# Products that nobody reads, between the score products of the first two groups of both attention layers

## The reference

```python
x = x + _L0_attn_ref(_layernorm(x), ...)   # delta rule, 4 heads
x = x + _L0_ffn_ref(x, ...)                # holds a softmax attention of 16 heads of 8, and a mixture of 8 experts
x = x + _L1_attn_ref(_layernorm(x), ...)   # softmax attention, 32 heads of 32
x = x + _L1_ffn_ref(x, ...)                # product with a spectrum
```

```python
attn = softmax(q @ k.T * scale)            # 512 x 512 scores for each batch entry and head
o = attn @ v
```

## Time and profile before

| | us |
|---|---|
| median of 3 runs | 2050.37 |
| lowest and highest | 2046.57, 2053.72 |
| the profiled execution, its own time | 2045.67 |
| its span, first to last instruction | 2044.0 |

### The profile page before, as it was taken

The page is one execution under the profiler, slowest core; times in us unless marked ns, Lnnn a source line. Parts: engine busy times, 40 slices in busy tenths (PEclk is TensorE's granted clock), DMA queues, the critical chain, the costliest instruction groups (busy, mean ns, idle before and its releaser), DMA issues. The chain is left out here.

```text
span 2044.0 us, 49130 instructions
## 1 busy us (share of the span) xinstructions
PE 1792.3 (88%) x18950; PEld 832.5 (41%) x18950; DVE 1630.1 (80%) x3036; ACT 1285.0 (63%) x2693; POOL 1148.6 (56%) x703
## 2 busy tenths in 40 slices
PE   5537755999999955986999999999999999999997
PEld 3337733233333334663442444443443444444334
DVE  7842276999999746446878999999999999999963
ACT  5412125588888811225884777787787877777785
POOL 8722472000000037331134988989999999989995
PEclk9769958699999965998997999999999999999998
DMA  2220018111111052117994232332323223232311
GB/s 48 36 49 3 0 45 278 39 44 48 44 43 48 22 184 54 47 49 246 368 405 150 65 84 69 80 79 69 85 64 84 73 76 84 65 85 65 83 28 42
DMA packets 194495, 180.21 MB, mean 88 GB/s; under 512 B 58743, under 2 KB 155127, under 8 KB 194055
## 3 DMA queue, kind: packets, MB, share of 16 engines
q1 hardware_dynamic: 185860, 170.01, 28.6%
q0 software_dynamic: 2944, 7.10, 1.1%
q10 hardware_dynamic: 5504, 0.73, 0.2%
HBM read 101.16 MB, written 75.26 MB: 86 GB/s over the span
## 5 line engine op out<-in xcount | busy, mean ns | idle before, releaser
L972 DVE TENSOR_REDUCE maxima_l<-max_l 128x1 f32<-128x512 f32 x1024 | 651.6, 677 | 46.6 <-PE max_l L1082 40.3
L948 POOL TENSOR_TENSOR part_sums_l<-probs_l 128x1024 f32<-128x1024 f32 x256 | 615.1, 2403 | 98.3 <-ACT probs_l L1038 85.4
L1038 ACT ACTIVATE probs_l<-exp_l 128x512 f32<-128x512 f32 x1024 | 567.9, 598 | 139.6 <-PE exp_l L1093 135.5
L1082 PE MATMUL max_l<-k_stack_l,q_stack_l 96*128 96x512 f16 x1024 | 399.4, 391 | 4.1 <-DVE pv_bank_l L964 3.3
L1093 PE MATMUL exp_l<-q_stack_l,k_stack_l 100*128 100x512 f16 x1024 | 389.8, 382 | 2.5 <-ACT probs_l L1038 1.6
L1300 DVE TENSOR_REDUCE maxima_l<-max_l 128x1 f32<-128x512 f32 x512 | 316.9, 681 | 16.9 <-PE max_l L1386 16.7
L1337 ACT ACTIVATE probs_l<-exp_l 128x512 f32<-128x512 f32 x512 | 279.2, 599 | 59.6 <-PE exp_l L1399 55.9
L1127 PE MATMUL pv_bank_l<-probs_l,v_ring_l 128*32 128x512 f32 x2048 | 273.6, 606 | 0.3 <-issue 0.3
L1814 POOL IOTA rows_e<- 128x32 int32 x1 | 0.2, 183 | 386.1 <-POOLq L26 386.1
L1082 PEld LDWEIGHTS max_l<-k_stack_l,q_stack_l 96*128 96x128 f16 x1024 | 100.1, 98 | 280.1 <-DVE maxima_l L972 189.1
L979 DVE TENSOR_TENSOR part_sums_l<-part_sums_l 128x512 f32<-128x512 f32 x128 | 182.5, 1426 | 14.2 <-POOL part_sums_l L948 14.1
(11 more groups left out here) (294 smaller groups left out, 2588.6 us busy)
## 6 DMA issues: line engine op xcount, KB each, us to landing
scratch_qk_l<-parts_g SPq DMA_DIRECT2D x128, 256.0 KB, 9.3
q_stack_l<-scratch_qk_l SPq DMA_DIRECT2D x192, 128.0 KB
k_stack_l<-scratch_qk_l SPq DMA_DIRECT2D x192, 128.0 KB
scratch_v_l<-v_g SPq DMA_DIRECT2D x16, 1024.0 KB, 11.2
v_ring_l<-scratch_v_l SPq DMA_DIRECT2D x64, 256.0 KB, 3.4
scratch_stack_l<-parts_c SPq DMA_DIRECT2D x16, 384.0 KB, 3.6
q_stack_l<-scratch_stack_l SPq DMA_DIRECT2D x64, 96.0 KB, 2.2
k_stack_l<-scratch_stack_l SPq DMA_DIRECT2D x64, 96.0 KB, 2.3
```

Source lines behind the costliest of these rows:

```text
L948: pool.tensor_tensor(part_sums[:, i, h, :, :], probs[:, i, h, 0:2, :], probs[:, i, h, 2:4, :], ALU.add).then_inc(pair_sum.sem, 1)
L972: dve.reduce_max(maxima[:, s % 2, at % NT, at // NT:at // NT + 1], max_bank(n, at)[:, :], AX).then_inc(max_taken.sem, 1)
L1038: act.activation(probs[:, i, at // NT, at % NT, :], exp_ps[at % 2][:, :], ACT.Exp, scale=a.scale).then_inc(prob_tile.sem, 1)
L1082: pe.matmul(max_bank(n, at)[:, :], qs[0:SHIFT_ROW, s % RING, h, k * P:(k + 1) * P], ks[0:SHIFT_ROW, s % RING, h, :], start=True, stop=True ...
```

## The change

In steps 0 and 1, behind each score for the maxima, TensorE makes products of 384 columns from the same stacks and writes them into `exp_ps`. Nobody reads them. In L1 there are two behind each score, 64 in all. In L0 there are four behind each pair of scores, 64 in all, and all of them read the rows 0 to 47, whichever half the scores read. In L0 they count a semaphore of their own, `filled`, and TensorE waits for all 64 ahead of the first score for the exponentials. I call them fill products below.

```diff
+IDLE_FILL, IDLE_WIDTH = 2, 384
 # attention (L1), in the loop over the 16 tiles, if exists(turn, s, 0):
                         pe.matmul(max_bank(n, at)[:, :], qs[0:SHIFT_ROW, s % RING, h, k * P:(k + 1) * P],
                                   ks[0:SHIFT_ROW, s % RING, h, :], start=True, stop=True).then_inc(max_tile.sem, 1)
+                        if not exists(turn, s, EXP_LAG):
+                            for f in range(IDLE_FILL):
+                                pe.matmul(exp_ps[f % 2][:, 0:IDLE_WIDTH], qs[0:SHIFT_ROW, s % RING, h, k * P:(k + 1) * P],
+                                          ks[0:SHIFT_ROW, s % RING, h, 0:IDLE_WIDTH], start=True, stop=True)
 # attention_l0 (L0), in the loop over the 8 pairs
+        filled = sem("filled")
...
+                        if not exists(turn, s, EXP_LAG):
+                            for f in range(2 * IDLE_FILL):
+                                pe.matmul(exp_ps[f % 3][:, 0:IDLE_WIDTH], qs[0:L0_ROWS, s % RING, hh, k * P:(k + 1) * P],
+                                          ks[0:L0_ROWS, s % RING, hh, 0:IDLE_WIDTH], start=True, stop=True).then_inc(filled, 1)
                     if exists(turn, s, EXP_LAG):
                         m, slot = n - EXP_LAG, (s - EXP_LAG) % RING
                         if p == 0:
                             pe.wait_ge(shifted[slot], nth(turn, s - EXP_LAG, 16 * HALVES * NT))
+                            if not exists(turn, s, EXP_LAG + 1):
+                                pe.wait_ge(filled, 2 * IDLE_FILL * EXP_LAG * L0_PAIRS)
```

## The result

| | us | |
|---|---|---|
| before | 2049.56 | median of 11 runs (2046.57 to 2053.72) |
| after | 2058.15 | median of 11 runs (2053.71 to 2062.81) |
| ratio | 1.0042 | 95% interval 1.0031 to 1.0054: 6.4 to 11.1 us slower |
| profiled execution of after | 2059.5 | span 2057.8 (before: 2044.0) |

What follows compares the result with a forecast made beforehand. VectorE was taken to bound both layers' starts, TensorE at the low clock some later stretches. L0 (1.2 + 0.4 - 1.7 = -0.1) plus L1 (1.8 - 0.6 = +1.2) gave +1.1 us: 2051.5 from 2050.37, range 2046 to 2060.

Steps and rivals of the forecast that it cites:

- the first rival: L0: clock stays low despite the fill products, as they use 48 of 128 rows; +9.6 us, 2060.0; chance 0.13.
- The bound: Steps 0 and 1 of both layers: VectorE's reductions set the pace at 0.60 us a tile, not TensorE.
- The price of a tile or pair: TensorE with fill products at 0.50: 1.70 us an L0 pair, 1.06 an L1 tile; at 1.00, 0.55 a tile.
- how long L0's clock stays low: Start of L0: 4.2 us until the rise (ends 2.4 and 6.0), so 2.5 pairs late by 0.50, +1.2 us.
- The gain in L0: L0, start of step 3: with the clock high from step 2, VectorE's 1.93 us gap shrinks to 0.21, returning 1.7 us.
- a sign against me: Forecast wrong if the clock falls back in step 1, stays 0.50 in L0, or reductions stand over 0.60 apart at 1.00.
- the fourth rival: Larger gain: before's low clock may last longer elsewhere, about a microsecond per further L0 step 3 pair; about 2043; chance 0.04.
- the 0.6 that I took: L1, step 2: a high clock gives back the 0.6 us by which VectorE was short in 4.2.
- the bound of 1.7: L1, step 2: upper limit on the gain, TensorE's 11.3 us against 9.6 for 16 tiles.
- The shift's chain: Transposed maxima of group 0 queue behind fill products: about 0.4 us shows in L0 (0 to 0.66), nothing in L1.
- The second rival: Fill products' weight loads not overlapped: L1 tile 0.85 us at the high clock; +8.1 us in all, 2058.5; chance 0.01.
- The third: Rival: the clock rises in neither layer before step 2; 8.0 us lost in L0, 14.7 in L1, 2073; chance 0.02.

Runs made afterwards that it cites:

- l0_narrow: Kernel after without L1's fill products, L0's made 192 columns wide instead of 384, still 48 rows: 2049.8 us against 2048.64 for before, one run.
- fitted: Kernel after with one 192-column fill product per L1 tile; L0's only in step 2, one of 128 rows per pair, pairs 3 to 7: 2046.82 us against 2045.09, ratio 1.0003.
- fitted_all: As fitted, but L0's 128-row fill products stand behind all eight pairs of step 2: 2047.1 us, one run.
- l1_narrow: Kernel after without L0's fill products; in L1 one of 192 columns behind each score instead of two of 384: 2045.32 us against 2045.54, ratio 0.9995.
- l0_alone: Kernel after with L1's fill products taken out, L0's kept: 2056.84 us against 2045.94 for before, ratio 1.0054.
- l0_rows48: Kernel after without L1's fill products; L0's read 48 rows of a separate tile filled once by ScalarE: 2060.05 us against 2045.94 for before, one run.
- l1_rows48: Kernel after without L0's fill products; L1's use 48 rows instead of 96: 2068.6 us against 2048.64 for before, one run.
- l1_alone: Kernel after with L0's fill products and their wait taken out, L1's kept: 2047.29 us against 2045.94 for before, ratio 1.0008.
- l0_rows128: Kernel after without L1's fill products; L0's read all 128 rows of a separate tile filled once by ScalarE: 2048.78 us against 2045.94, one run.
- l0_halves: Kernel after without L1's fill products; L0's alternate between lower and upper 48 rows, 512 columns each: 2047.64 us against 2048.64 for before, one run.
- l0_bridge: l0_rows128 plus two 128-row fill products per pair through step 2 and a wait for them before step 3: 2045.1 us against 2045.54, one run.
- keep_warm: Kernel before plus unread float32 products ending the stage ahead, 15 before L0 and 5 before L1; none in the attentions: 2054.25 us against 2048.64, one run.

## Why the prediction was right and wrong

**The number was inside by way of a rival.** 2058.15 us is above the forecast's own 2048 to 2055. The range reached it only because its upper end was put at the price of the first rival, which had a chance of 0.13. Of the forecast's own mechanism, L1's part came about, with one term too small, and L0's part did not.

**The bound was read rightly.** VectorE at 0.60 us a tile bounds steps 0 and 1 of both layers. The runs whose fill products kept TensorE under that at the low clock lost nothing there (l0_narrow, and fitted, fitted_all and l1_narrow in L1), and after, l0_alone, l0_rows48 and l1_rows48, which went above it, lost time pair by pair or tile by tile.

**The price of a tile or pair was right.** Forecast at 0.50: 1.70 us a pair in L0 and 1.06 a tile in L1; measured 1.71 and 1.07. Forecast at 1.00: 0.55 in L1; measured 0.55. Both come from the two spacings of scores in the earlier trace rows.

**The step that failed is how long L0's clock stays low.** I wrote "I take 4.2 us, as that is the same kind of product, with 2.4 and 6.0 as ends". For L1 it held: 5.4 us in after, 3.5 in l1_alone. (The 4.3 us beside it was misread: with 0.71 in the earlier trace rows the clock rises at 938.6, 4.5 us behind 934.12. Nothing hangs on it.) For L0 it was the wrong row. L1's scores use 96 and 100 rows, L0's fill products 48, and with these the clock was 0.50 through all 16 pairs: 16 x 0.50 = 8.0 us instead of 2.5 x 0.50 = 1.2, and 8.3 measured at the first exponentials' score. The nearest row of the same width was L0's own step 2, 10 us at 0.50. I named it in the rival and set it aside, because that step leaves both halves of the array idle a third of the time. In after and l0_rows48 there were no gaps, and the clock stayed low just as well; in l0_rows128 it rose in 3.3 us, once the same products used 128 rows. So gaps were not what held it down in after. With a row for 48 rows that spoke against me and none that spoke for me, 0.13 was too low.

**The gain in L0 failed for a second reason.** The 1.7 us supposed that a clock raised in steps 0 and 1 stays up through step 2. In l0_rows128 and l0_halves it rose and fell back in step 2, and gaps of 1.65 and 1.71 us stayed. I had listed a fall back in step 1 as a sign against me, and not one in step 2, though the earlier trace rows show step 2's own products at 0.50. l0_bridge shows the size of the gain to be right, if the clock is held. The reverse is seen in after: the low clock lasted longer in step 3 and cost a second gap of 0.96 us, near the microsecond a pair that the fourth rival put on it.

**L1 came out about even, with a term mis-sized.** Forecast: +1.8 at the low clock, -0.6 returned. The first exponentials' score comes 21.2 us behind the first score in after (1108.7 - 1087.5) where it was 19.2, +2.0, and 20.1 in l1_alone, +0.9. From the first to the last exponentials' score L1 takes 2000.7 - 1094.8 = 905.9 us in before and 904.6 in after and l1_alone, -1.3. This difference is steady: 905.6 to 905.9 in the nine kernels without 96-row fill products in L1, 904.3 to 904.6 in the five with them. So what comes back is twice the 0.6 that I took, and under the bound of 1.7 that I gave. VectorE was indeed busy in all the rest of step 2 (7.00 of 7.00 us from 1099 to 1106), but some of the gain lies behind it: its first wait for the partial sums of POOL is 0.66 us in before and 0.24 in after. Together it makes +0.7 in after and -0.4 in l1_alone; the second is within what unchanged layers differ by.

**The shift's chain** can't be told apart in after, where everything in step 1 is late anyway. In the runs with a high clock in step 1 VectorE's gap at the start of step 2 was 0.22 us in l0_bridge and nothing in l0_rows128 and l0_halves. That is within the 0 to 0.66 that I gave, and below my 0.4.

**The first rival's sum** was +9.6. The profiled executions give 9.4 + 0.7 = 10.1 for the two layers, the medians 8.6. Its price was right, its chance was not. **The second rival**, weight loads in the open, is out: with its fill products L1's tile took 0.55 us at 1.00, as it would with every load hidden, and not 0.85. The Trainium skill, "TensorE: Matmul & The Clock Gate", section "Part 3: Packing small matmuls", says in one place that loads overlap only products of other row groups, and this row disagrees with that too. In another place the same section also lets a load go ahead into a background weight buffer; that was left out of the prediction, and the rows do not speak against it. **The third**, no rise in either layer, is out by L1's rise after 5.4 us. **The fourth**, a larger gain, is out by the sign.

**What stays open.** Fill products between 48 and 96 rows weren't tried. It isn't known why two halves of 48 rows together took 10 us to bring the clock up, nor why 96-row products took 3.5 to 5.9 us at the low clock in three executions and about 14 in two others (l1_narrow and fitted_all, both with narrow fill products; fitted had the same ones and is among the three). Between l0_rows128 and fitted both the place and the share of the 128-row products differ, so which of the two kept the clock low in fitted is open. The loss itself doesn't hang on these: that the clock was low and that the overrun at the low clock is the loss are both measured. No kernel tried here is faster than before by more than can be measured.

## What to carry to other kernels

Filler work that is to raise TensorE's clock runs at the low clock first, and may never get out of it: cost it at the low clock against the engine that bounds the stage, and make it narrow enough to fit there. Then being wrong about the clock costs next to nothing, as l0_narrow shows beside after. Take the time to a rise only from stretches whose products use as many rows, and not from a single one, since the same products took 5.9 and 13.6 us here (fitted, l1_narrow); and ask of each place between the fill and the gain whether its own work keeps the clock. When a change moves the whole by less than its scatter, the length of each layer in the trace still tells the parts apart.

## What I had not expected of the hardware

- Gapless work alone didn't raise the clock: 27.0 us of 48-row products in after and 38.9 us of 96-row scores with 48-row fill products in l1_rows48 ran at 0.50, where products of 96 and 128 rows were at 1.00 after 3.3 to 5.9 us in five executions and after some 14 us in two.
- The clock fell from 1.00 to 0.50 while TensorE was busy again: 1.4 us into L1 in l1_alone, where the 3.4 idle us ahead of L1 had passed at 1.00, and 1.5 to 1.8 us into it in l1_rows48, l1_narrow and fitted_all. Whether it is the idle stretch that brings this fall, late, wasn't tried: in keep_warm, which was to fill the idle stretch, the clock fell too, but under bare scores.
- Changing between products of 48 rows and of more cost time of its own. With 48-row scores and 128-row fill products the first pair of l0_rows128 took 357.35 - 355.41 = 1.94 us instead of 1.70; with 96-row scores and 48-row fill products a tile of l1_rows48 took 1.30 instead of 1.06. Both are 0.24 us for a change there and back at the low clock. The Trainium skill, "TensorEngine Tiling (Array Packing)", section "Key Properties", says that changing the tiling mode drains TensorE; if that is what a change of the row count does here, the runs agree, and put a number to it.
- A float32 product of 128x128 by 128x512 took 0.87 us in keep_warm (15 of them 13.04 us), and so the 15 ran past the idle time of 8.7 us that they were to fill.
